# Two expert layers with routing by chunks of 512 tokens, a fixed region of rows per expert, and 23 unrolled slots

## What is computed

```python
x = x + attention_a(layernorm(x), W_K, W_Q, W_V, W_O)   # 16 heads of 64, causal softmax
x = x + experts(layernorm(x), w_red, wg, w1, b1, w2, b2)
x = x + attention_b(layernorm(x), ...)                  # 16 heads of 8, linear attention
x = x + experts(layernorm(x), w_red, wg, w1, b1, w2, b2)  # the same weights again

def experts(x, w_red, wg, w1, b1, w2, b2):              # 8 experts, 128 -> 512 -> 128
    logits = (x @ w_red) @ (wg / norm(wg)).T
    gates = softmax(logits, axis=1)
    idx = argmax(gates, axis=1)                          # one expert for each token
    h = gelu(x @ w1[idx] + b1[idx])
    return (h @ w2[idx] + b2[idx]) * gates[idx]
```

## Time and profile before

| | |
|---|---|
| median of three runs | 1361.99 us |
| the profiled execution | 1360.53 us, span 1358.8 us, granted clock 0.944 |
| busy share of the span | PE 86%, PEld 63%, DVE 70%, ACT 58%, POOL 61% |
| attention a | from the start to about 1019 us |
| first expert layer | about 1019 to 1127 us |
| linear attention | about 1127 to 1246 us |
| second expert layer | about 1246 us to the end |

### The profile page before, as it was taken

One profiled execution on the slowest core, in us unless ns is written; L12 is line 12 of the kernel. 1 busy time (PEld: TensorE's weight loads), 2 busy tenths in 40 slices (PEclk: granted clock), 3 DMA queues, 4 the chain that ended last, 5 costly groups with the idle time before them and its releaser, 6 DMA issues. The chain is left out here.

```text
span 1358.8 us, 24424 instructions
## 1 busy us (share of the span) xinstructions
PE 1173.5 (86%) x7936; PEld 855.3 (63%) x7936; DVE 957.3 (70%) x2108; ACT 794.6 (58%) x2192; POOL 829.2 (61%) x813
## 2 busy tenths in 40 slices
PE   5999999999999999999999999999973585885285
PEld 4666667676767767676676667676753582443285
DVE  5878677867776786878677777867743355998254
ACT  6777576767757775766677576766721342322053
POOL 0675668757866775887576768757852443552433
PEclk9899999999999999999999999999995796998588
DMA  4950200200020011002000200200000221000023
GB/s 124 125 141 16 48 1 1 52 12 1 1 63 1 1 32 32 1 1 63 1 1 8 57 1 1 50 14 1 1 1 17 57 61 32 1 0 1 29 60 98
DMA packets 52689, 41.18 MB, mean 30 GB/s; under 512 B 14177, under 2 KB 41442, under 8 KB 52578
## 3 DMA queue, kind: packets, MB, share of 16 engines
q1 hardware_dynamic: 50018, 34.50, 11.9%
q0 software_dynamic: 2560, 5.26, 1.2%
HBM read 13.49 MB, written 9.48 MB: 17 GB/s over the span
## 5 line engine op out<-in xcount | busy, mean ns | idle before, releaser
L325 POOL TENSOR_SCALAR at_prob<-at_prob,at_scale 128x512 f32<-128x512 f32 (+1 forms) x480 | 656.2, 1383 | 5.6
L353 DVE TENSOR_REDUCE at_nmax<-at_ps 128x1 f32<-128x512 f32 (+3 forms) x640 | 375.9, 603 | 154.1 <-PE at_ps L519 150.5
L434 ACT ACTIVATE at_prob<-at_ps,at_nmax 128x512 f32<-128x512 f32 (+3 forms) x640 | 393.1, 623 | 44.6 <-DVE at_nmax L353 43.7
L530 PE MATMUL at_ps<-ident,at_prob 128*128 128x128 f32 x2176 | 328.7, 275 | 23.4 <-DVE at_probT L376 19.1
L530 PEld LDWEIGHTS at_ps<-ident,at_prob 128*128 128x128 f32 x2176 | 255.7, 140 | 110.5 <-issue 52.6
L516 PE MATMUL at_ps<-at_k_st,at_q_parts 128*128 128x512 f32 (+3 forms) x640 | 285.1, 445 | 6.1 <-ACT at_prob L434 3.6
L448 ACT ACTIVATE at_probT<-at_ps 128x512 f32<-128x512 f32 (+1 forms) x288 | 165.1, 573 | 212.2 <-PE at_ps L530 188.0
L545 PE MATMUL at_ps<-at_probT,at_v 128*64 128x256 f32 (+1 forms) x2304 | 270.1, 374 | 12.3 <-DVE at_probT L376 12.3
L519 PE MATMUL at_ps<-at_k_st,at_q_parts 128*128 128x512 f32 (+3 forms) x640 | 253.1, 396 | 0.0
L376 DVE COPY at_probT<-at_ps 128x512 f32<-128x512 f32 (+1 forms) x288 | 189.0, 656 | 68.1 <-PE at_ps L530 64.7
L545 PEld LDWEIGHTS at_ps<-at_probT,at_v 128*64 128x64 f32 x2304 | 155.2, 136 | 107.1 <-issue 48.5
(11 more groups left out here) (189 smaller groups left out, 1364.1 us busy)
## 6 DMA issues: line engine op xcount, KB each, us to landing
at_q_parts<-at_q_parts SPq DMA_DIRECT2D x64, 256.0 KB, 3.5
f_xs<-slots_in SPq DMA_DIRECT2D x48, 64.5 KB
slots_in<-zeros SPq DMA_DIRECT2D x2, 1536.0 KB, 19.4
wall<-in_L_ffn_w_dram SPq DMA_DIRECT2D x1, 2048.0 KB, 19.8
wall<-in_L_ffn_w_dram SPq DMA_DIRECT2D x4, 512.0 KB, 6.1
f_got<-slots_out SPq DMA_DIRECT2D x8, 256.0 KB, 3.6
out_dram<-x SPq DMA_DIRECT2D x4, 256.0 KB, 2.4
slots_out<-f_ys,f_back POOLq DMA_INDIRECT x48
```

Source lines behind the costliest of these rows:

```text
L325: pool.tensor_scalar(cols, cols, scale[:, k, u, c:c + 1], None, ALU.mult).then_inc(s_fix["pool"], 1)
L353: dve.tensor_reduce(nmax[:, j % 2, u % 4, c:c + 1], bank, AX.X, ALU.max, negate=True).then_inc(s_max, 1)
L434: act.activation(prob[j % 2][u % 4][:, c * BANK:c * BANK + w], ring[use_of["score", p, u, c] % RING][:, 0:w], ACT.Exp, bias=nmax[:, j % 2, ...
L530: last = pe.transpose(turn_ps[h][:, b * P:(b + 1) * P], prob[j % 2][2 * i + h][:, t * P:(t + 1) * P], ident[:, :])
```

## The change

- **Regions.** slots_in grows from 3072 rows to 8 x 2048 + 7 x 128 = 17280 rows of 129 words. Expert e's tokens start at row 2048 e, whatever the counts. A token's row is therefore known from the one-hot tables of its own chunk and the chunks in front of it.
- **Gating, places and scatters by chunk.** Scores lie in a bank for each chunk. The ranks of chunk c are summed in PSUM by 9 + 4c small matmuls in bf16 (L936 to L942 after the change): the region's start, the counts of earlier tiles, and the rank inside the tile. VectorE needs three instructions for a chunk's rows (L805 to L808), and GpSimd scatters a chunk when `s_pos` has reached it.
- **Gate matrix.** It is kept from the first expert layer and not built again in the second, whose order of work is another one too (norm, choose and place alternate).
- **Slots.** 23 slots, fully unrolled, with eight load buffers. As a slot's rows now start at a row that depends on the counts, VectorE works out `slot_row` (L840 to L842), and SyncE loads it into a register before each slot's load. Unused rows are recognized by zero instead of by written numbers: an instruction that takes the larger of two numbers (L869) replaces two copies (L829, L835), and `sem_inc(s_ready)` on GpSimd goes.
- **Zeroing.** Both tensors are zeroed whole, 516 bytes a row. The work is cut into six pieces: after the last q_parts copy of pairs 1 to 6, SyncE issues two DMAs (one for each tensor) of 22 or 23 tiles, or 22.5 x 128 = 2880 rows on average. The weights are loaded where the zeroing stood, in pair 0.

The diff, cut to its core:

```diff
-        self.SLOTS = -(-(self.NT + self.E - 1) // 4) * 4
+        self.SLOTS = self.NT + self.E - 1
...
-                    if p == 0 and c == NC - 1:
-                        fetch(sp)
+                    if c == NC - 1:
+                        fetch(sp, p)
...
+                sp.wait_ge(s_slot, 2)
                 sp.wait_ge(s_scat, 16 * NT)
...
-                skewed(sp, SLOTS, U, {"load": 0}, emit)
+                for s in range(SLOTS):
+                    k = s % LOADED
+                    if s >= LOADED:
+                        sp.wait_ge(s_ys, s - LOADED + 1)
+                    row = sp.value_load(slot_row[0:1, s:s + 1], min_val=0, max_val=E * T + (E - 2) * P)
+                    sp.dma_start(xs[k][:, :], scratch_in[bass.ds(row, P), :]).then_inc(s_xs[k], 16)
...
-                pool.wait_ge(s_pos, 1)
                 for t in range(NT):
+                    pool.wait_ge(s_pos, t // TPC + 1)
                     pool.indirect_dma_start(scratch_in[:, :], ...)
...
+                def choose(c):
+                    rows = slice(TPC * c, TPC * (c + 1))
+                    dve.wait_ge(s_lg, c + 1)
+                    link(dve.tensor_reduce(lmax[:, rows], logits(c), AX.X, ALU.max))
...
+                def find_place(c):
+                    dve.wait_ge(s_rank, c + 1)
+                    link(dve.tensor_tensor(place[:, c, :, :], ranks(c)[:, :, 0:TPC], onehot[:, c, :, :], ALU.mult))
+                    rows = slice(TPC * c, TPC * (c + 1))
+                    link(dve.tensor_reduce(pos[:, rows], place[:, c, :, :].rearrange("p e t -> p t e"), AX.X, ALU.add))
+                    dve.tensor_copy(pos_u[:, rows], pos[:, rows]).then_inc(s_pos, 1)
...
+                def rank(c):
+                    pe.wait_ge(s_hot, c + 1)
...
+                    pe.matmul(ranks(c), keep["all"][0:1, :], keep["region"][:, :, :], start=True, stop=False)
+                    for d in range(c):
+                        for t in range(TPC):
+                            pe.matmul(ranks(c), keep["all"][:, :], onehot[:, d, :, t:t + 1].to_broadcast([P, E, TPC + 1]), start=False, stop=False)
+                    for t in range(TPC):
+                        pe.matmul(ranks(c)[:, :, t:t + 1], keep["before"][:, :], onehot[:, c, :, t:t + 1], start=False, stop=False)
+                        last = pe.matmul(ranks(c)[:, :, t + 1:TPC + 1], keep["all"][:, :], onehot[:, c, :, t:t + 1].to_broadcast([P, E, TPC - t]),
+                                         start=False, stop=t == TPC - 1)
...
-    def fetch(sp):
+    def fetch(sp, p):
+        if 1 <= p <= PIECES:
+            sp.wait_ge(s_z, 1)
+            for scratch in scratch_ins:
...
+                a, b = n * (p - 1) // PIECES, n * p // PIECES
+                sp.dma_start(rows[:, a:b, :], keep["zeros"][:, :].unsqueeze(1).to_broadcast([P, b - a, D + 1])).then_inc(keep["s_scratch"], 16)
```

More of the change, by code:

```diff
@@ new lines, in _ @@
+                if make_gate:
+                    for c in range(NC):
+                        norm(c)
+                        gate_weights(c)
+                    choose(0)
+                    for c in range(1, NC):
+                        choose(c)
+                        find_place(c - 1)
+                else:
+                    norm(0)
+                    for c in range(1, NC):
+                        norm(c)
+                        if c + 1 < NC:
+                            statistics(c + 1)
+                        if c >= 2:
+                            find_place(c - 2)
+                        choose(c - 1)
+                    find_place(NC - 2)
+                    choose(NC - 1)
@@ L803, in _ @@
+                find_place(NC - 1)
+                count = ranks(NC - 1)[:, :, TPC:TPC + 1]
+                link(dve.tensor_tensor(over[:, :, :], count.to_broadcast([P, E, NT]), keep["full"][:, :, :], ALU.is_gt))
                 link(dve.tensor_reduce(tiles[:, :], over[:, :, :], AX.X, ALU.add))
                 link(dve.tensor_tensor_scan(ends[:, :], keep["ones8"][:, :], tiles[:, :], 0.0, ALU.mult, ALU.add))
-                link(dve.tensor_tensor(starts[:, :], ends[:, :], tiles[:, :], ALU.subtract))
@@ L858, in _ @@
-                act.wait_ge(s_sub, 1)
-                act.activation(ex[:, :, :], sub[:, :, :], ACT.Exp).then_inc(s_ex, 1)
-                def emit(stage, turn, c):
-                    s, k = U * turn + c, c % U
+                    if not make_gate and c:
+                        act.wait_ge(s_xnTp, c)
+                        act.activation(xnT[:, (c - 1) * BANK:c * BANK], ps[(c - 1) % 2][:, :], ACT.Copy).then_inc(s_xnT, 1)
+                for c in range(0 if make_gate else NC - 1, NC):
+                    act.wait_ge(s_xnTp, c + 1)
+                    act.activation(xnT[:, c * BANK:(c + 1) * BANK], ps[c % 2][:, :], ACT.Copy).then_inc(s_xnT, 1)
@@ L887, in _ @@
-                pe.wait_ge(s_gate, 1)
-                for t in range(NT):
-                    pe.wait_ge(s_xnT, t // TPC + 1)
-                    last = pe.matmul(lg[:, t, :], xnT[:, t * P:(t + 1) * P], gate[:, :], start=True, stop=True)
-                last.then_inc(s_lg, 1)
-                pe.wait_ge(s_hot, 1)
-                hot = onehot[:, :, :].rearrange("p e t -> p (e t)")
-                pe.matmul(rank_ps[:, 0:E * NT], keep["before"][:, :], hot, start=True, stop=True)
-                pe.matmul(rank_ps[:, E * NT:2 * E * NT], keep["all"][:, :], hot, start=True, stop=True).then_inc(s_rank, 1)
@@ L897, in emit, with turn @@
-                def emit(stage, turn, c):
-                    s, k = U * turn + c, c % U
-                    first = static_tile(turn, c) is not None and c < 2
+                def turn(c):
+                    if c >= 2:
+                        pe.wait_ge(s_xnT, c - 1)
+                    for t in tiles_of(c):
+                        pe.wait_ge(s_xn, t + 1)
+                        last = pe.transpose(ps[c % 2][:, t % TPC * P:(t % TPC + 1) * P], xn[:, t, 0:D], ident[:, :])
+                    last.then_inc(s_xnTp, 1)
@@ new lines, in _ @@
+                turn(0)
+                if make_gate:
+                    pe.wait_ge(s_gin, 16)
+                    pe.transpose(gateT_ps[:, 0:D], wred[:, :], ident[:, :])
+                    pe.wait_ge(s_wgn, 1)
+                    pe.transpose(gateT_ps[:, D:D + E], wgn[:, :], ident[0:E, 0:E]).then_inc(s_wgTp, 1)
+                    turn(1)
+                    pe.wait_ge(s_wgT, 1)
+                    pe.matmul(gate_ps, wredT[:, :], wgnT[:, :], start=True, stop=True).then_inc(s_gateP, 1)
+                    turn(2)
+                    turn(3)
+                    pe.wait_ge(s_gate, 1)
+                    for c in range(NC):
+                        score_experts(c)
+                        if c:
+                            rank(c - 1)
+                else:
+                    for c in range(1, NC):
+                        turn(c)
+                        score_experts(c - 1)
+                        rank(c - 1)
+                    score_experts(NC - 1)
@@ L900, in emit @@
+                rank(NC - 1)
+                if beside:
+                    pe.wait_ge(beside["tensor"](pe, ps[4]), 1)
+                def emit(stage, s, k):
                     if stage == "xT":
-                        pe.wait_ge(s_xs[k], 16 * (turn + c // U + 1))
-                        if not first:
+                        pe.wait_ge(s_xs[s % LOADED], 16 * (s // LOADED + 1))
+                        if s >= 2:
                             pe.wait_ge(s_xsT, s - 1)
-                        pe.transpose(ps[c % 2][:, 0:P], xs[k][:, 0:D], ident[:, :]).then_inc(s_xsTp, 1)
+                        pe.transpose(ps[s % 2][:, 0:P], xs[s % LOADED][:, 0:D], ident[:, :]).then_inc(s_xsTp, 1)
```

244 lines of the change are left out of this document (122 added, 122 removed).

## The result

| | before | changed |
|---|---|---|
| median of the runs, us | 1362.08 (1359.45 to 1362.51, 4 runs) | 1342.26 (1341.89 to 1343.67, 4 runs) |
| profiled execution, us | 1360.53 | 1342.05 |
| its span, us, granted clock | 1358.8, 0.94 | 1340.2, 0.947 |

The ratio is 0.9864, with a 95% interval of 0.9848 to 0.988: 19.8 us between the medians where 17.7 were forecast. The forecast of 1344.3 is 2.0 us too long, and its range holds the time. Under the sum, two groups of terms were off and largely made up for each other.

What follows compares the result with a forecast made beforehand. Each expert layer was taken to pay gating plus scatters in series, then slots bound by TensorE. -6.3 - 11.1 - 3.8 + 2.5 + 1.0 = -17.7 gave 1342.8 profiled, 1344.3 us as median, range 1337 to 1353.

Steps and rivals of the forecast that it cites:

- Scatters of layer 1: Layer 1 gating: scatters start by chunk at 1035.5, and the last ends at 1055.7 instead of 1062.0 us, -6.3 us.
- The ranking matmul at 0.11 us: Gating on TensorE: each small bf16 ranking matmul takes 0.11 us, so a chunk's ranks cost 1.0 to 2.3 us.
- Scatters of layer 2: Layer 2 gating: first scatter at 1258.6 instead of 1270.88, last ending at 1280.0 instead of 1291.13 us, -11.1 us.
- late wake-ups: Layer 2 scatters: GpSimd, barely fed between chunks, wakes late twice, an allowance of 1.1 us.
- The rival in which it starves: Layer 2: ranking matmuls cost 0.213 us, GpSimd waits for place 3, and the time is 1351 us; chance 0.13.
- A slot less: Expert slots: leaving out the 24th saves 1.89 us of TensorE in each layer, -3.8 us.
- My rival on the clock: Start of the slots: TensorE's clock rises early after denser gating and a shorter idle stretch, 1338 us; chance 0.10.
- Register loads: SyncE, start of the slots: register loads delay the first w1 multiply by 1.25 us a layer, +2.5 us in all.
- Zeroing, 0: Attention: zeroing 17280 rows in two tensors, six pieces of about 36 us, costs 0, at most 0.9 us.
- scatters beside VectorE: Gating: up to 12 of 16 scatters run beside VectorE's instructions and slow by 0.5 us a layer, +1.0 us.
- the rival of slow scatters: Gating: all 12 scatters of both layers take 1.18 us, costing 5.3 instead of 1.0, so 1348.6 us; chance 0.10.
- The other rivals: Register load sets slot rhythm (0.03, 1367 at 2.4 us); zeroing disturbs attention (0.04, 1362); change does less (0.02, 1360.7).

Runs made afterwards that it cites:

- the repetition: The changed kernel measured once more with nothing edited: 1343.73 us, ratio 0.9873 to the kernel before.

## Why the prediction was right, and where its steps were not

- **Scatters of layer 1, -6.3.** The last scatter ends 8.6 us earlier, and 7.35 earlier when both are measured from the stage's start. The first started at 1032.89, 14.9 behind the start, where I had 16.2, and the whole 1.3 lies in front of the scores: chunk 0's are ready at about 1028.5, 10.5 behind the start instead of 11.8. The gate product (1024.53) was 0.5 us earlier than I had it, and the last two chunks were transposed in 1.97 us, for which I had 2.5 and waits. The chain from there, in part:

```profile
1025.05 1.97 PE L921 MATMUL f_ps<-ident,f_xn 128*128 128x128 f32 x8
...
1026.81 3.42 PE L929 MATMUL f_ps<-gate,f_xnT 128*128 128x8 f32 x16
...
1030.16 0.21 PE L936 MATMUL f_ps<-region,all 1*128 1x40 bf16 x1
...
1030.52 0.17 PE L942 MATMUL f_ps<-f_onehot,all 128*128 128x8 bf16 x1
...
1031.17 0.23 DVE L800 TENSOR_TENSOR f_onehot<-f_prio,f_best 128x32 bf16<-128x32 f32 x1
1031.28 0.18 DVE L805 TENSOR_TENSOR f_place<-f_ps,f_onehot 128x32 f32<-128x32 f32 x1
```

  The ranking matmul at 0.11 us was wrong as well, but not on this path: rank 0 took 0.5 us instead of 1.0 and was ready at 1030.69, and place 0 stands behind choice 1, which ended at 1031.40. A weight load reads 0.10, but the loads overlap (twelve in 0.46 us from 1036.11), and the matmuls follow each other every 0.03 us even at 1.2 GHz, so rank 3 took 0.9 us (1035.97 to 1036.89) instead of 2.3:

```profile
1035.97 0.21 PE L936 MATMUL f_ps<-region,all 1*128 1x40 bf16 x1 [0.54 <-DVE f_onehot L800]
1036.11 0.58 PE L939 MATMUL f_ps<-f_onehot,all 128*128 128x40 bf16 x12
...
1036.72 0.17 PE L942 MATMUL f_ps<-f_onehot,all 128*128 128x8 bf16 x1
```

- **Scatters of layer 2, -11.1.** Measured from the stage's start, the last ends 13.05 us earlier. The first came 11.5 us behind the start, where my timeline had 12.2, and the last places 22.0 behind it instead of 27.2. The four ranks took 2.9 us instead of 6.6, which is most of these 5.2. The 1.1 us for late wake-ups were not needed: GpSimd never waits. The rival in which it starves fell with the same number.
- **A slot less, -3.8.** Right as a price (1.7 to 2.0 a layer at equal clock), wrong as a result: this is the term that failed. From the first load to the read-back 0.1 us came in both layers together, where this term less the second register loads had 2.5. My rival on the clock asked whether it would rise early; that it could rise later than before, and cost as much as the slots bring, I did not have.
- **Register loads, +2.5.** From last scatter to first load +0.73 and +0.67, and another 0.46 and 0.49 to the first w1 multiply: +2.4 in all. SyncE's row, against the earlier trace rows:

```profile
L715 SPq TENSOR_LOAD <-f_slot_row x46: 262/268/477, 1054.8 to 1311.8; - x46
L715 SPq FUSED_REGOPS  x46: 152/152/187, 1055.3 to 1312.1; - x46
```

  The Trainium skill's floor of about 600 ns ("DMA: Bandwidth & Descriptors", Latency and other measured facts) does not hold for these loads: 268 ns. With four of them ahead of the wait the price is gone.
- **Zeroing, 0, and scatters beside VectorE, +1.0.** The first holds within what can be told; a piece's two DMAs landed 16.4 and 15.6 us after their issue, where I reckoned 36 for the two. The second was 0.25 in layer 1 (20.50 instead of 20.25) and -0.06 in layer 2; so the rival of slow scatters fell. A single one shows it: 1.32 us at 1041.96, begun while VectorE's copy of the weights ran (1041.69, 0.76 us). The Trainium skill ("GPSIMD Engine Reference", 8. Key points) says that GpSimd shares its SBUF interfaces with VectorE and contends with instructions in a 2-port mode or with two SBUF inputs. That would fit this scatter and the stores that end behind the copy, but the copy reads one input and no row tells its mode, so no run here isolates it.
- **The other rivals.** The register load does not set the rhythm (1.89 as before), and the change does what it says. The copies of q_parts of the pair shown started at 128.95 and 254.10 instead of 130.32 and 255.48, and the attention ended at 1018.03, ahead of my limit of 1019. That limit was too narrow to tell anything: in the repetition it ended at 1019.30, just as in the kernel before.
- **The sum.** In front of the loads I had 15.2 us (17.4 less 1.2 for the first register load and 1.0 for slower scatters), and 19.0 came. In the slots I had 2.5 (3.8 less 1.3 for the second register load), and 0.1 came. 3.8 too few and 2.4 too many nearly cancelled; the linear layer and the end add 0.4 net of the attention. The linear layer itself, which the change leaves alone, took 118.6 to 120.8 us in these profiles, so this part is chance. The forecast's mechanism for most of the gain was right, its closeness partly luck.

What stays open: why the clock rises early or late. It was late in 7 of 18 layers whose second transpose follows the first by more than 0.9 us, and in none of the 6 in which it follows sooner, the kernel before among them. For a link speaks that the five runs with four early registers lie within 2.0 us; against it, that 15 runs of the kernel before, which is of the same group, spread over 6.0 (1359.27 to 1365.29). 6 layers are few, and the same code did both.

## What to carry to other kernels

A serial stage of one engine, here GpSimd's scatters, is best attacked by giving it its first input early; it needs its chunks only as fast as it can use them. When a change shortens the wait before a TensorE stage, look at the granted clock of that stage's first 10 us on both sides, since its first instructions can run at half speed for longer and pay back a whole saved iteration. And look at what starts behind the wait: registers, tables and the clock could all be made ready during it, and together that was worth 11 us here.

## What I had not expected of the hardware

- TensorE's clock rose anywhere from 3.3 to 10.7 us behind the first slot, in one execution of the same code after 10.7 in one layer and 3.6 in the other.
- TensorE lost the upper level, which 14 us of multiplications had held, within an idle stretch of 3.6 us: at 1057 to 1058 us its mean is 0.65, and from 1058 on 0.50.
- Bf16 matmuls of 8 to 40 columns with a new weight load each follow at 0.03 us, at 1.2 GHz.
- GpSimd's indirect store takes anything from 0.96 to 1.39 us: where VectorE's copy of 128x1156 begins 0.1 to 0.5 us into it, it ends about 0.12 us behind the copy. An increment of a semaphore in front of it moves it out of that range.
